# Five bulk loads issued from the scalar engine, and softmax scratch given buffers of its own, in a five-layer attention kernel

## What is computed

```python
x = LN(x + self_attention(x))                        # "sa"
x = LN(x + cross_attention(x, ctx, s % 4 == h % 4))  # "ca": each head sees a quarter of the keys
x = LN(x + gelu(x @ W1) @ W2)                        # "f"
a = attention(x @ Wq, ctx @ Wkv, key mask)           # "l1"
x = LN(x + [x, a @ Wo] @ Wu)
x = LN(x + causal_attention(x, ctx))                 # "l2"
x = x + gelu(x @ V1) @ V2                            # "g"
w = relu(scores)**2 where |s - index[b, t]| <= 1     # "l3", keys and values of rmsnorm(ctx)
out = x + (w / max(sum(w), eps)) @ v @ Wo
```

## Time and profile before

| | us |
|---|---|
| median of 3 runs (lowest to highest) | 394.14 (393.71 to 397.4) |
| the profiled execution's own time | 388.13 |
| its span, first to last instruction | 386.3 |
| PE busy | 302.8 (78%) |
| PE weight loads busy | 220.1 (57%) |
| DVE busy | 165.5 (43%) |
| ACT busy | 157.2 (41%) |
| POOL busy | 56.1 (15%) |

### The profile page before, as it was taken

One profiled execution on the slowest core, in us unless ns is written; L12 is line 12 of the kernel. 1 busy time (PEld: TensorE's weight loads), 2 busy tenths in 40 slices (PEclk: granted clock), 3 DMA queues, 4 the chain that ended last, 5 costly groups with the idle time before them and its releaser, 6 DMA issues.

```text
span 386.3 us, 9704 instructions
## 1 busy us (share of the span) xinstructions
PE 302.8 (78%) x4055; PEld 220.1 (57%) x4055; DVE 165.5 (43%) x348; ACT 157.2 (41%) x380; POOL 56.1 (15%) x75
## 2 busy tenths in 40 slices
PE   4447109999979694467969998799899989998493
PEld 3346005777967573246835776356655667777273
DVE  5997007424485730561077844233213222343251
ACT  4990000236543531629481454222441156455131
POOL 7702001500016310030200000000000000100000
PEclk9755555559985786559995598555665599899556
DMA  7935651100220245025522101146410001100301
GB/s 251 248 68 73 82 76 30 45 5 5 70 57 11 51 74 87 11 30 66 68 71 70 32 4 39 48 61 85 73 37 3 2 18 31 42 16 11 86 3 29
DMA packets 25565, 20.95 MB, mean 54 GB/s; under 512 B 3377, under 2 KB 21554, under 8 KB 25266
## 3 DMA queue, kind: packets, MB, share of 16 engines
q1 hardware_dynamic: 24706, 19.60, 25.2%
q0 software_dynamic: 816, 0.73, 1.5%
HBM read 4.61 MB, written 0.52 MB: 13 GB/s over the span
## 4 chain that ended last, share of the span: by engine, by line
PE 63%; DMA 11%; SPq 9%; DVE 7%; ACT 6%; issue 4%; POOL 0%; ACTq 0%; POOLq 0%
PE bank L560 18%; PE s_bank L682 13%; PE t_bank L732 10%; DMA k_stack_sb<-k_part_sb 9%; PE bank L798 7%; PE s_bank L560 7%; SPq L524 5%; SPq L489 4%; PE t_bank L560 4%; PE bank L774 3%; DVE k_part_sb L1136 2%; DMA cst_sb<-in_consts 1%; ACT k_part_sb L899 1%; PE bank L694 1%; DVE k_part_sb L1132 1%
## 5 line engine op out<-in xcount | busy, mean ns | idle before, releaser
L1067 DVE TENSOR_REDUCE m_col_sb<-s_bank 128x8 f32<-128x512 f32 (+1 forms) x52 | 35.7, 687 | 76.6 <-PE s_bank L682 75.3
L682 PE MATMUL s_bank<-k_stack_sb,q_stack_sb 96*64 96x128 bf16 (+1 forms) x384 | 51.5, 412 | 19.2 <-DMA k_stack_sb<-k_part_sb 18.4
L682 PEld LDWEIGHTS s_bank<-k_stack_sb,q_stack_sb 96*64 96x64 bf16 (+1 forms) x384 | 25.7, 143 | 39.1 <-issue 26.8
L732 PEld LDWEIGHTS t_bank<-q_stack_sb,k_stack_sb 102*128 102x128 bf16 (+1 forms) x512 | 36.7, 163 | 13.4 <-issue 13.0
L928 ACT ACTIVATE probs_sb<-t_bank 128x512 f32<-128x512 f32 x52 | 29.9, 604 | 31.3 <-PE t_bank L732 29.3
L732 PE MATMUL t_bank<-q_stack_sb,k_stack_sb 102*128 102x64 bf16 (+1 forms) x512 | 41.7, 240 | 0.0
L1262 POOL TENSOR_SCALAR vare_sb<-var_sb 128x2 f32<-128x2 f32 x20 | 5.8, 291 | 207.9 <-ACT q_rest_sb L972 207.9
L560 PE MATMUL bank<-v_ext_sb,probs_sb 128*32 128x18 f32 (+1 forms) x2112 | 33.3, 206 | 1.7 <-ACT probs_sb L928 0.8
L560 PEld LDWEIGHTS bank<-v_ext_sb,probs_sb 128*32 128x32 f32 (+1 forms) x2112 | 29.2, 133 | 9.2 <-issue 8.2
L774 PE MATMUL bank<-W_sb,q_rest_sb 128*128 128x128 f32 x80 | 19.7, 334 | 11.3 <-DVE q_rest_sb L1094 5.9
L560 PE MATMUL bank<-xa_sb,W_sb 128*128 128x256 f32 x56 | 19.7, 474 | 8.6 <-DMA W_sb<-in_mats 4.3
(11 more groups left out here) (140 smaller groups left out, 537.4 us busy)
## 6 DMA issues: line engine op xcount, KB each, us to landing
q_stack_sb<-q_part_sb SPq DMA_DIRECT2D x120, 64.0 KB, 2.6
k_stack_sb<-k_part_sb SPq DMA_DIRECT2D x48, 128.0 KB
W_sb<-in_mats SPq DMA_DIRECT2D x1, 1152.0 KB, 8.5
W_sb<-in_mats SPq DMA_DIRECT2D x1, 1024.0 KB, 10.6
ctxT_sb<-in_ctxT SPq DMA_DIRECT2D x1, 512.0 KB, 6.2
hid_sb<-in_ctx SPq DMA_DIRECT2D x1, 512.0 KB, 13.3
out<-q_full_sb SPq DMA_DIRECT2D x4, 128.0 KB, 1.9
xa_sb<-in_xT SPq DMA_DIRECT2D x1, 384.0 KB, 4.7
```

Source lines behind the costliest of these rows:

```text
L682: last = pe.matmul(o[64 * c:64 * c + 64, s4 * 128:(s4 + 1) * 128], q_stack[0:r, g, s, t:t + T], keys(k_stack[STACK[name]], r, s, b), start ...
L732: last = pe.matmul(o[:, s * T:(s + 1) * T], keys(k_stack[STACK[name]], r, s, b), q_stack[0:r, g, s, i * T:(i + 1) * T], start=not masked, ...
L1067: dve.tensor_reduce(o, s_bank[turn("s", name, g, i)[0]][:, :].rearrange("p (c k) -> p c k", k=w), AX.X, ALU.max).then_inc(sem("max"), 1)
```

## The change

Five loads (`ctxT`, w2, `cn`, w3 and the index row, in that order) leave SP's list and stand ahead of everything on ACT; before, w3 stood ahead of `cn`. The key mask stays on SP. `ctx_sq` becomes a bf16 buffer of its own, and `dist` is computed in place in the index row's buffer, inside `relu`. The waits and the dependencies of the exponentials of "sa" on the band mask and the squares go. In the changed program every line behind the removed loads has a number that is smaller by 6, and from line 930 of the old program on by 3.

```diff
@@ timetable
-                p = add("act", .5, "exp", name, g, i, after=[t] + ([band, cms] if name == "sa" else []))
+                p = add("act", .5, "exp", name, g, i, after=[t])
@@ build
-        ctx_sq = probs[:, 2:4, :].rearrange("p a n -> p (a n)")
+        ctx_sq = sb("ctx_sq", [128, B // 2, 128], BF)
...
-        dist = probs[0:64, 0:2, :].rearrange("p a n -> p (a n)")
+        dist = relu[0:64, :, :].rearrange("p a n -> p (a n)")
@@ block.sync
-            sp.dma_start(ctxT[:], a["ctxT"]).then_inc(sem("ctx_loaded"), 16)
-            sp.dma_start(W[:, FIRST_MATS:NEXT_MATS, :], a["mats"][:, FIRST_MATS:NEXT_MATS, :]
-                         ).then_inc(sem("w2_loaded"), 16)
-            sp.dma_start(W[:, NEXT_MATS:, :], a["mats"][:, NEXT_MATS:, :]).then_inc(sem("w3_loaded"), 16)
-            sp.dma_start(cn, a["ctx"].rearrange("(n p) d -> p n d", p=128)).then_inc(sem("cn_loaded"), 16)
-            sp.dma_start(idx, a["idx"].to_broadcast([64, TOK])).then_inc(sem("idx_loaded"), 16)
@@ block.scalar, exps
-                else:
-                    act.wait_ge(sem("band"), 1)
-                    act.wait_ge(sem("ctx_ms"), 1)
@@ block.scalar, ahead of its steps
+            act.dma_start(ctxT[:], a["ctxT"]).then_inc(sem("ctx_loaded"), 16)
+            act.dma_start(W[:, FIRST_MATS:NEXT_MATS, :], a["mats"][:, FIRST_MATS:NEXT_MATS, :]
+                          ).then_inc(sem("w2_loaded"), 16)
+            act.dma_start(cn, a["ctx"].rearrange("(n p) d -> p n d", p=128)).then_inc(sem("cn_loaded"), 16)
+            act.dma_start(W[:, NEXT_MATS:, :], a["mats"][:, NEXT_MATS:, :]).then_inc(sem("w3_loaded"), 16)
+            act.dma_start(idx, a["idx"].to_broadcast([64, TOK])).then_inc(sem("idx_loaded"), 16)
```

More of the change, by code:

```diff
@@ L950, in _ @@
                     for n in range(B // 2):
-                        last = act.activation(ctx_sq[:, n * 128:(n + 1) * 128], cn[:, n, :], ACT.Square,
+                        last = act.activation(ctx_sq[:, n, :], cn[:, n, :], ACT.Square,
                                               scale=D ** -0.5, accum_out=cms[:, n:n + 1])
```

## The result

| | changed kernel | kernel before, beside it | ratio, 95% interval |
|---|---|---|---|
| first measurement | 403.0 us (400.07 to 406.91, 4 runs) | 393.92 us | 1.0378 [1.0243, 1.0513] |
| second | 400.89 us (396.86 to 406.98, 4 runs) | 394.34 us | none given |
| third | 402.37 us (398.73 to 404.34, 6 runs) | 393.75 us | 1.0229 [1.0166, 1.0291] |

The forecast was 396.1 us with a range up to 402.0. The third measurement has the narrowest interval, so I take the loss as 2.3%, that is 9 us (6.5 to 11.5). The profiled execution of the changed kernel took 405.57 us with a span of 403.3; those of the second and third measurement took 398.85 and 398.73.

A forecast was written before the change was run, and what follows sets the result against it. It took a chain of constants, DVE, SP and transfers to bound the first 58 us, then PE to 134, then the second key stack. +3.8 − 5.0 + 3.2 = +2.0 on 394.14 gave 396.1 us, range 389 to 402.

The forecast's parts named there:

- Constants late: Start: constants on SP share full DMA engines with ACT's `ctxT` and w2, so land later: +4.0 us, bounds 0 to +4.0.
- ACT's five issues: Start: ACT is free only at 9.0 us after issuing the loads, but DVE starts later too: 0.
- SP's stall: SP's twelve query issues: POOL's transfer stalls them, shorter without bulk loads beside it: −1.7 us, bounds 0 to −1.8.
- "ca" transfers in the stack: POOL's twelve "ca" key transfers fall into the "sa" key stack's transfer: +1.5 us, bounds 0 to +5.7.
- first scores: PE's first scores, the sum of the start's terms: +3.8 us, at about 61.9.
- PE between 58 and 134: Work taken from ahead of `k.l1.g3` brings it and the "l1" key stack earlier: −5.0 us, bounds −7.3 to −2.
- Behind the second key stack: "ca" pieces taken out wait behind the "l1" stack, partly filling PE's gaps: +3.2 us, bounds 0 to +5.8.
- Removed waits and scratch: Removed waits, scratch, key mask and bf16 squares: not on the path ahead of the first exponentials, 0.
- Rival B: "ca" transfers choke the "sa" key stack (over 32 us) and SP's stall stays: +7.9, 402.0 us; chance 0.18.
- Rival C: `k.l1.g3`'s gain is given back in full behind the stack, only the start counts: +3.8, 397.9 us; chance 0.15.
- rival A: Constants not late, PE's 2.3 us gap closes and full clock lasts longer: −6.5, 387.6 us; chance 0.27.
- the table load near 179: Sign of a right forecast: the table load, with which the hidden layer starts, stands near 179 us.

The follow-up runs named there:

- rows_late: Kernel before, with POOL's transfers of constant rows moved behind its work on the squares of the context: 392.6 us beside 393.75, ratio 0.9921.
- old_order: Changed kernel with the "sa" exponentials again depending on band mask and squares, so every engine runs the order of before: 396.29 us, ratio 1.0057.
- old_loads: Changed kernel with the five loads back on SP in their old places, the changed order of steps kept: 399.31 us, ratio 1.0121.
- fixed_order: Changed kernel with the five loads back on SP and the first operation of the maxima's parts by TENSOR_TENSOR: 395.19 us, ratio 0.994.
- no_clash: Changed kernel with the first operation of the maxima's parts written as TENSOR_TENSOR (zeros minus maximum) instead of TENSOR_SCALAR: 398.42 us, ratio 1.0028.
- km_first: Changed kernel with the two key-mask transfers ahead of the twelve "l1" key transfers on SP again: 401.55 us, ratio 1.0164.
- m_on_act: Changed kernel with the four transfers of the "ca" maxima's rows issued by ACT instead of SP: 402.35 us, ratio 1.0197.
- before again: Kernel before, unchanged, run once more with a second profile: 394.29 us, its profiled execution 397.25 us.
- Two edits: On the kernel before: POOL's constant rows later (0.9921), and key transfers issued by the part they carry (0.9935); both together 379.57 us, ratio 0.9642.

## Why the prediction was wrong

The direction of the sum was right (+2.0 us), the size was not (+9). By its own steps, with the changed kernel's three profiles against the two of before:

- **Constants late, +4.0:** 2.8, inside its bounds. The weights of SP's list were late too, which I had not priced; PE and ACT had the room.
- **ACT's five issues, 0:** right. They were over at 5.69, not 9.0; the table load at 8.82 waited for PE, and DVE's run has no wait for ACT in it.
- **SP's stall, −1.7:** wrong in size. The cause was named rightly (rows_late), but POOL's transfer was still there, so 14.41 us of 15.00 stayed. The assumption that it would be shorter without bulk loads beside it failed; only 0.6 us went.
- **"ca" transfers in the stack, +1.5:** first issue to first scores is 31.5, 30.4 and 30.2 us against 29.1 and 29.1 before, so 1.1 to 2.4. Right; old_order, where they stand behind the stack, has 29.2 and old_loads, where they stand in it, 30.9. Together first scores came at +3.4 to +5.2, forecast +3.8.
- **PE between 58 and 134, −5.0:** this is the step that failed. It said that `k.l1.g3` *and the key stack of "l1" behind it* come 5.0 earlier, since PE is the limit. From first scores to `k.l1.g3` it is 71.7 and 73.7 us in before and 70.8, 68.0 and 68.0 in the changed kernel, 3.8 less on the mean. But to the first issue of the stack it is 76.9 and 79.3 against 78.5, 76.1 and 76.1, only 1.2 less. Two things stood in the way.
  - DVE's wait behind POOL's memsets. In fixed_order and no_clash, where DVE does not wait, `k.l1.g3` comes after 63.6 us, 9 less than in before. I counted PE's work that leaves the way and bounded DVE only by its own load; what I did not look up is what DVE would run beside POOL's memsets in the new order.
  - SP's list. `k.l1.g3` to the first key issue grew from 5.2 and 5.6 us to 7.7, 8.1 and 8.1. SP's six query issues of "ca" group 3 (136.82 to 141.02) now stand ahead of the keys whose last part was ready at 139.12, so 1.9 of it is SP; in no_clash, where POOL's transfer stalls them, it is 5.1. I had read from the order that the keys come earlier and not that SP's list puts a query group ahead of them. That is read from the traces; no run has the list put right.
- **Not in the sum at all:** the transfer takes 29.3 us to ACT's next work instead of 27.5, with the key-mask rows and two maxima's rows behind it. km_first and m_on_act, which move these rows, have 28.5 and 28.4, so these rows are 0.9 of the 1.8 at most; the rest stays open.
- **Behind the second key stack, +3.2:** 23.3, 21.6 and 21.7 us against 20.0 and 21.5, so +1.5 on the mean. Smaller than forecast, though old_order's 19.8 and old_loads' 23.4 leave room for it.
- **Removed waits and scratch, 0:** nothing here contradicts it; old_order, which has them, shows no more than its late start.

The first scores (+4.2), −3.8, +2.6, +1.8 and +1.5, all as means (the stack of the quick execution left out), give +6.3. That is just below the lower end of the measured loss, 6.5 us, with a scatter of 2 us each way; two of the three profiled executions of the changed kernel lie 3.6 us under its median of 402.37. That the late start and DVE's wait are enough to make the loss is shown by fixed_order, which has neither and is level with before. SP's list is unchanged there, and what PE gains covers it: from first scores to the first key issue it takes 74.0 us, against 76.9 and 79.3 in before.

Rival B's number (402.0) was met, but by luck and not by its mechanism: the first stack took 31.5 us, under the 32 that it needed. Rival C came nearest in kind: what `k.l1.g3` gains (3.8) is given back behind it (2.6, 1.8 and 1.5), only that I had put the place of it behind the stack alone. Of rival A, the gap did close (PE's wait of 2.3 us for a maximum is in no profile with the changed order), but the clock hardly gained by it: from first scores to `k.l1.g3` it is 0.71 to 0.73 in no_clash, fixed_order and the second and third profile, against 0.69 and 0.66 in before and 0.71 in old_order.

The base was weak as well: I set the forecast on the median, but read the stages behind 134 us from an execution that lay 6.0 us below it. Its second stack took 22.1 us, and 5.4 of the 9.1 us between the profiled executions of before and before again are that stack. The sum does not use the 22.1 us, but the table load near 179, by which the forecast was to be known as right, rests on them.

## What to carry to other kernels

Where a change reorders work, look for each short operation on the path not only at what stands ahead of it on its own engine, but at what POOL runs at that moment (0.18 us became 4.8 here), and at the list of the engine that issues the transfer: keys that are ready early gain nothing while SP still issues queries. Small urgent loads on one queue and bulk loads on another share the DMA engines, and here a single queue in the right order brought the constants 2.8 us earlier. When the profiled execution is over 1% off the median, find the place where it differs before taking durations from there.

## What the runs showed that was not expected

- A TENSOR_SCALAR of 128x32 took 4.77 to 4.85 us beside POOL's memsets in every profile with the changed order and this form, and 0.15 to 0.18 elsewhere; TENSOR_TENSOR with both inputs in SBUF was not held. Casts were held too, in the order of before only until the running memset ended.
- SP's issues stall while POOL's 128 KB transfer of constant rows is out: 15.00 against 7.70 us for twelve, 10.76 against 3.83 for six, with the bulk loads on SP in all four. Beside the second such transfer, six query issues of the changed order take 7.39 instead of 4.20.
- Two edits worth 0.8% and 0.65% alone are worth 3.6% together, all by the ratios.
- The 2 KB packets of a key stack took some 205 ns in one execution, and 242 to 280 ns in all other stacks that I measured. What made the one quick stays open.
